# Queries and keys of an attention stage stacked through DRAM: stores of 128 partitions and loads per band in place of copies of 32 partitions

## The chip, the cores and the metric

The kernel runs on one core of a Trainium2 chip. TensorE (PE in the rows) multiplies, VectorE (DVE), ScalarE (ACT) and GpSimd (POOL) work on the elements, and SyncE (SP) issues all DMAs of the kernel from one queue. The metric is the device time of one execution in microseconds.

## The reference, cut to what matters

```python
x = x + tanh(g_xattn[0]) * xattn(layernorm(x), ctx, ctx, mask, ...)
x = x + tanh(g_ffn[0]) * ffn(layernorm(x), W_r, W_k, W_v, mu_r, mu_k)

def xattn(query, key, value, attn_mask, ...):      # B 8, S 512, D 512, 16 heads of 32
    Q, K, V = proj(query, q_w, q_b), proj(key, k_w, k_b), proj(value, v_w, v_b)
    scores = einsum('bhqd,bhkd->bhqk', Q, K) / sqrt(32)
    attn = softmax(where(attn_mask, -1e9, scores), axis=-1)
    ctx = einsum('bhqk,bhkd->bhqd', attn, V)
    return einsum('bsd,ed->bse', heads_joined(ctx), o_w) + o_b

def ffn(x, W_r, W_k, W_v, mu_r, mu_k):
    xr, xk = mu_r * x + (1 - mu_r) * x_prev, mu_k * x + (1 - mu_k) * x_prev
    return sigmoid(xr @ W_r.T) * (square(relu(xk @ W_k.T)) @ W_v.T)
```

All is float32.

## The kernel before, in words

The kernel has two stages: attention for all eight batches, then output projection and feed-forward part. The change is in the first.

A batch has four *windows* (c = 0 to 3), one for each group of four heads. A window has 16 *tiles*, and TensorE, VectorE and ScalarE each go through it in 16 *steps*: tile i = 4 * head + block of 128 queries. For each tile TensorE computes 128 x 512 scores (`scores`, L502), VectorE adds the mask and takes the row minimum (L857), ScalarE exponentiates (L681), TensorE transposes the result (L509) and VectorE or ScalarE copies it out. After the 16 steps come the context matmuls of the group (L521) and a transpose of the reciprocals (L491). `scores` runs two tiles ahead: at step 14 TensorE computes the first tile of the *next* group, and at the window's end the third.

Between the steps TensorE does *side* work by a table written by hand (`PE_SIDE`): the projections Q (L476), K (L476), V (L485) for coming groups and the transposes of x. In window 0 the parts of K for the next group stand at steps 0, 1, 3 and 4, in window 1 too, in window 2 at steps 5, 6 and 7, in window 3 at steps 0 to 2. Q for the group after the next stands at the end of a window. In window 0 the next batch's x is also loaded (L300), and VectorE takes its statistics.

Matmuls are float32r, and float32 precision is won by splitting each operand in a high and a low part. ScalarE makes the high part (`q_hi`, `k_hi`, 128 partitions for four heads x 32, and 512 columns; L670), VectorE the low part (`q_lo`, `k_lo`; L845). For scores the parts are *stacked* along the contraction: for each head a stack of 96 partitions in three bands of 32, in Q high, high, low, and in K high, low, high, so that one matmul adds the three products. There are two sets of stacks (`stack[n % 2]`). They are filled by SP: `stack_rows` (L331) copies 32 partitions of a part into one band of one head, 64 KB each, 24 copies for a group. `stacked` counts them for each head apart, and `scores` waits for a head's count at the head's first tile only (L498 to L500). `qk_hi` and `qk_lo` have no second buffer: ScalarE waits for all copies of a group before it writes the next group's part (L653, L654).

All of this stands on SP in one order, with the waits written in it:

```python
for c in range(GROUPS):
    if c == 0 and not is_last(b):
        sp.wait_ge(side_done, ...); load_x(b + 1)      # 1 MB, L300
    if c:
        store_context(b, c - 1)                        # 256 KB to DRAM, L383
    ...
        sp.wait_ge(s_mm, tile_no(b, c, 0) + HEAD)
        stack_group(b, c + 1)                          # 24 copies, L331
    if c == 0 and not is_last(b):
        load_ctx(b + 1)                                # 1 MB, L303
```

Of the kernel before, what the change touches and what calls it, by code (L numbers as in the profile page):

```python
# [25 lines left out]
P = 128  # L26
# [60 lines left out]
EARLY = LO_STEP + 1  # L87

# [17 lines left out]
STACK_DMAS = 3  # L106
# [10 lines left out]
def build(nc, x, ctxT, mask, g_xattn, g_ffn, wq, bq, wk, bk, wv, bv, wo, bo, wr, wkk, wvv, mur, muk, ident_d, out,  # L117
          ctx_dram):
# [10 lines left out]
    with keep:  # L129
# [89 lines left out]
        stacked = [[sem(f"{n}_stacked_head{j}") for j in range(GH)] for n in "qk"]  # L219
# [19 lines left out]
        def side_no(b, item):  # L239

            if b is None:
                return PROLOGUE.index(item)
            order = ORDER_LAST if isinstance(b, int) and b == B - 1 else ORDER
            return b * SIDE_PER_BATCH + len(PROLOGUE) + order.index(item)

        def side_bank_of(b, item):
            if b is None:
                return side_bank[PROLOGUE.index(item) % SIDE_BANKS]
            order = ORDER_LAST if isinstance(b, int) and b == B - 1 else ORDER
            return side_bank[(len(PROLOGUE) + order.index(item)) % SIDE_BANKS]  # L250

        def mm_no(b, item):

            order = PROLOGUE if b is None else ORDER_LAST if isinstance(b, int) and b == B - 1 else ORDER
            at = [i for i in order if i[0] != "C"].index(item)
            return at if b is None else b * MM_PER_BATCH + MM_PROLOGUE + at

        def hi_no(b, item):

            if b is None:  # L260
                return [i for i in PROLOGUE if i[0] != "V"].index(item)
            order = [i for i in (ORDER_LAST if isinstance(b, int) and b == B - 1 else ORDER) if i[0] != "V"]
            return b * HI_PER_BATCH + HI_PROLOGUE + order.index(item)
# [14 lines left out]
        def is_last(b):  # L278
            return isinstance(b, int) and b == B - 1
# [18 lines left out]
        def _(sp):  # L298
# [65 lines left out]
            stack_k(None, 0, range(GH))  # L364
            for j in range(GH):
                stack_q(None, 0, (j,))
# [18 lines left out]
            def batch(b):  # L385
                for c in range(GROUPS):
# [26 lines left out]
            for b in range(B - 1):  # L413
                batch(b)
            batch(B - 1)
# [14 lines left out]
            for b in range(B - 1):  # L430
                step2(b, 0)
                step2(b, 1)
            step2(B - 1, 0)
            step2(B - 1, 1)
# [5 lines left out]
        def _(pe):  # L440
# [124 lines left out]
            def transposes(b, h):  # L565
                u = b * 2 + h
                if isinstance(b, int) and b + h == 0:
# [10 lines left out]
            for b in range(B - 1):  # L578
                batch(b)
            batch(B - 1)  # L580
# [52 lines left out]
            for b in range(B - 1):  # L633
                step2(b, 0)
                step2(b, 1)
            step2(B - 1, 0)
            step2(B - 1, 1)
# [3 lines left out]
        def _(act):  # L641
# [4 lines left out]
            def side(b, kind, n):  # L646
# [67 lines left out]
            def early_steps(b):  # L714

                for i in range(EARLY):
                    tile_step(b, 0, i)
                    if i == HI_STEP and b:
                        side(b - 1, "R", GROUPS - 1)

            def batch(b):
                for c in range(GROUPS):
                    for i in range(EARLY if c == 0 else 0, TILES):
                        tile_step(b, c, i)
                        if is_last(b) and (c, i) in SPLIT_W2:
# [9 lines left out]
                if not is_last(b):  # L735
                    early_steps(b + 1)
# [5 lines left out]
            def context_hi(b, h):  # L742
                act.wait_ge(c2_ld[h], b * 16 + 16)
                if isinstance(b, int) and b + h == 0:

                    for copied in (*stacked[0], *stacked[1]):
                        act.wait_ge(copied, B * GROUPS * STACK_DMAS * 16)
# [3 lines left out]
            early_steps(0)  # L751
            for b in range(B - 1):
                batch(b)
            batch(B - 1)
# [42 lines left out]
            for b in range(B - 1):  # L797
                step2(b, 0)
                step2(b, 1)
            step2(B - 1, 0)  # L800
            step2(B - 1, 1)
# [3 lines left out]
        def _(dve):  # L805
# [104 lines left out]
            def early_steps(b):  # L910

                for i in range(EARLY):
                    tile_step(b, 0, i)
                    if i == LO_STEP and b:
                        side(b - 1, "R", GROUPS - 1)

            def batch(b):
                for c in range(GROUPS):
                    for i in range(EARLY if c == 0 else 0, TILES):
                        tile_step(b, c, i)  # L920
                        if c == 0 and i in STATS_STEPS and not is_last(b):
# [18 lines left out]
                if not is_last(b):  # L940
                    early_steps(b + 1)
# [5 lines left out]
            def residual1(b, h):  # L947
# [3 lines left out]
                if isinstance(b, int) and b + h == 0:  # L951
                    dve.wait_ge(consts, 3)
                if not (isinstance(b, int) and b == 0):
# [22 lines left out]
            early_steps(0)  # L976
            for b in range(B - 1):
                batch(b)
            batch(B - 1)
# [63 lines left out]
            for b in range(B - 1):  # L1043
                step2(b, 0)
                step2(b, 1)
            step2(B - 1, 0)
            step2(B - 1, 1)
# [3 lines left out]
        def _(pool):  # L1051
# [69 lines left out]
            for b in range(B - 1):  # L1121
                step2(b, 0)
                step2(b, 1)
            step2(B - 1, 0)
            step2(B - 1, 1)
# [39 lines left out]
```

## Time and profile before

| | |
|---|---|
| Time, median of 3 runs | 1234.52 us (1232.02 to 1234.85) |
| Profiled execution | 1232.68 us, of it span 1230.8 us |
| PE busy | 1167.7 us, 95% |
| DVE busy | 942.5 us, 77% |
| ACT busy | 745.2 us, 61% |
| POOL busy | 237.4 us, 19% |
| DMA moved | 110.33 MB, 90 GB/s on average |
| Chain that ended last | PE 76%, DVE 9%, issue 6%, ACT 4%, DMA 4% |
| Mean granted TensorE clock | 0.99 of full speed |

Busy is the time in which an engine had an instruction under way, as a share of the span. The chain is followed back from the last instruction, at each step to what released it. The times of all rows are microseconds from the span's start.

### The profile page before, as it was taken

To read this page: it belongs to the slowest core of one execution; us is meant where nothing else is said; L and a number is where in the kernel's file an instruction comes from. 1 tells how busy PE (TensorE), PEld (TensorE's weight loads), DVE (VectorE), ACT (ScalarE), POOL (GpSimd) and SP (SyncE) were. 2 spreads that over 40 slices of the span, in tenths; PEclk is the share of its full clock that TensorE was granted. 3 is DMA by queue.
4 is the path that set the end of the run, shared out by engine and by line. 5 is a ranking of instruction groups with operands and counts; after the bars stand their busy time and mean duration, and the time that the engine had idled before them with its cause. 6 is when DMAs were issued, how large, how long until landed. Compare 5 with 4: busy or idle time off the path is not lost.

```text
span 1230.8 us, 22178 instructions
## 1 busy us (share of the span) xinstructions
PE 1167.7 (95%) x7424; PEld 921.5 (75%) x7424; DVE 942.5 (77%) x2011; ACT 745.2 (61%) x1619; POOL 237.4 (19%) x427
## 2 busy tenths in 40 slices
PE   3999999999999999999999999977999999999997
PEld 2777776777777777777677777754888888888886
DVE  5778788788878887878878887879677677777763
ACT  4578778678768877877867876764432333233232
POOL 2030030030021003003003000024423433332431
PEclk9999999999999999999999999987999999999999
DMA  6433342253243333344225322452111311311200
GB/s 218 120 94 83 101 122 66 63 157 81 71 129 89 81 102 100 82 104 118 67 60 159 78 74 65 123 168 76 59 52 60 95 52 52 104 52 52 97 25 35
DMA packets 72703, 110.33 MB, mean 90 GB/s; under 512 B 14864, under 2 KB 23696, under 8 KB 72592
## 3 DMA queue, kind: packets, MB, share of 16 engines
q1 hardware_dynamic: 72592, 108.92, 31.1%
q8 instruction: 61, 1.00, 0.3%
q14 instruction: 50, 0.41, 0.1%
HBM read 41.76 MB, written 16.78 MB: 48 GB/s over the span
## 4 chain that ended last, share of the span: by engine, by line
PE 76%; DVE 9%; issue 6%; ACT 4%; DMA 4%; SPq 1%; POOL 0%; POOLq 0%; ACTq 0%; DVEq 0%
PE bank L445 24%; PE bank L509 14%; PE bank L476 12%; PE bank L521 10%; PE bank L502 7%; PE bank L485 6%; DMA x_rows<-x 3%; DVE neg_s L857 3%; ACT probs L681 2%; PE bank L491 2%; PE bank L575 1%; DVE pT L863 1%; DVE xh L973 1%; DMA pT<-wkT 1%; DVE ctx_sb L848 1%
## 5 line engine op out<-in xcount | busy, mean ns | idle before, releaser
L681 ACT ACTIVATE probs<-neg_s,negmax 128x512 f32<-128x512 f32 x512 | 367.9, 720 | 40.5 <-DVE negmax L857 39.4
L857 DVE CUSTOM_DVE_ANT_0 neg_s<-bank,mask_big 128x512 f32<-128x512 f32 x512 | 344.7, 683 | 19.2 <-PE bank L502 16.9
L509 PE MATMUL bank<-ident,probs 128*128 128x128 f32 x2048 | 314.8, 276 | 17.3 <-ACT probs L681 16.8
L509 PEld LDWEIGHTS bank<-ident,probs 128*128 128x128 f32 x2048 | 240.4, 141 | 75.6 <-ACT probs L681 40.7
L863 DVE COPY pT<-bank 128x512 f32<-128x512 f32 x256 | 176.5, 690 | 120.8 <-PE bank L509 119.7
L502 PE MATMUL bank<-k_stack,q_stack 96*128 96x512 f32 x512 | 243.3, 475 | 6.0 <-DVE negmax L857 5.9
L688 ACT COPY pT<-bank 128x512 f32<-128x512 f32 x256 | 149.4, 584 | 98.3 <-PE bank L509 92.5
L1068 POOL TENSOR_SCALAR var_eps<-mv 128x2 f32<-128x2 f32 (+1 forms) x24 | 18.5, 770 | 639.9 <-DVE mv L822 578.3
L521 PE MATMUL bank<-pT,v_sb 128*32 128x512 f32 x1024 | 118.5, 603 | 0.8 <-issue 0.5
L779 ACT ACTIVATE relu<-bank 128x512 f32<-128x512 f32 x32 | 19.2, 598 | 149.0 <-PE bank L445 149.0
L502 PEld LDWEIGHTS bank<-k_stack,q_stack 96*128 96x128 f32 x512 | 97.3, 190 | 11.2 <-DVE negmax L857 8.5
L681 ACT ACTIVATION_READ_ACCUMULATOR probs<-neg_s,negmax 128x1 f32 x512 | 97.3, 190 | 0.0
L521 PEld LDWEIGHTS bank<-pT,v_sb 128*32 128x32 f32 x1024 | 33.1, 111 | 69.8 <-issue 69.8
L1108 POOL TENSOR_TENSOR o_sb<-o_sb,x 128x1024 f32<-128x1024 f32 x16 | 39.1, 2444 | 173.5 <-DVE o_sb L1032 173.5
L1093 POOL TENSOR_TENSOR x_in<-x_in,tgbo 128x1024 f32<-128x1024 f32 x16 | 38.9, 2434 | 141.1 <-DMA x_in<-x 140.1
L1083 POOL TENSOR_SCALAR x_rows<-x_rows,mv,rstd 128x512 f32<-128x512 f32 x28 | 57.8, 2078 | 0.8
L476 PE MATMUL bank<-cT_lo,wk_hi 128*128 128x512 f32 x128 | 40.4, 418 | 17.2 <-DVE cT_lo L836 17.2
L672 ACT COPY ctx_sb<-bank 128x512 f32<-128x512 f32 x32 | 18.8, 589 | 62.4 <-PE bank L491 62.4
L1017 DVE TENSOR_TENSOR kact_lo<-kact,kact_hi 128x1024 fp32r<-128x1024 f32 x16 | 40.0, 2498 | 17.9 <-ACT kact_hi L781 17.9
L957 DVE SCALAR_TENSOR_TENSOR x<-bank,tg,x_in 128x512 f32<-128x512 f32 x32 | 23.9, 751 | 37.1 <-POOL o_sb L1108 35.9
L1014 DVE SCALAR_TENSOR_TENSOR kact<-bank,relu 128x512 f32<-128x512 f32 x32 | 22.1, 692 | 38.5 <-ACT relu L779 38.5
L485 PE MATMUL bank<-wv_hi,cT_lo 128*128 128x256 f32 x256 | 45.6, 282 | 0.0
(110 smaller groups left out, 2125.1 us busy)
## 6 DMA issues: line engine op xcount, KB each, us to landing
k_stack<-k_hi SPq DMA_DIRECT2D x256, 64.0 KB, 2.0
q_stack<-q_hi SPq DMA_DIRECT2D x256, 64.0 KB, 2.0
x_rows<-x SPq DMA_DIRECT2D x8, 1024.0 KB, 6.6
cT_raw<-ctxT SPq DMA_DIRECT2D x8, 1024.0 KB, 5.8
k_stack<-k_lo SPq DMA_DIRECT2D x128, 64.0 KB, 2.0
q_stack<-q_lo SPq DMA_DIRECT2D x128, 64.0 KB, 2.0
ctx_dram<-ctx_sb SPq DMA_DIRECT2D x32, 256.0 KB, 2.1
c_raw<-ctx_dram SPq DMA_DIRECT2D x16, 512.0 KB, 5.1
```

The costliest lines, as they stand in the source:

```text
L445: mm = nc.tensor.matmul(dst, lhs(left, a), rhs(right, a), start=(part == 0 and a == 0), stop=(part == TERMS - 1 and a == CH - 1))
L476: mm = nc.tensor.matmul(bank[:], left[:, at % CH, cols], right[:, at % CH, :], start=(at == 0), stop=(at == TERMS * CH - 1))
L485: mm = nc.tensor.matmul(bank[:, k * UNIT:(k + 1) * UNIT], left[:, a, keys * P:(keys + 1) * P], right[:, a, n // 2 * UNIT:(n // 2 + 1) * UNIT],
L502: nc.tensor.matmul(s_bank[i % S_BANKS][:], stack[slot][0][:, j, q * P:(q + 1) * P], stack[slot][1][:, j, :], start=True, stop=True).then_i ...
L509: mm = nc.tensor.transpose(pt_bank[i % 2][:, a * P:(a + 1) * P], probs[:, i % P_RING, a * P:(a + 1) * P], ident[:])
L521: nc.tensor.matmul(pv_bank[j * HD:(j + 1) * HD, :], v_sb[:, a, head * HD:(head + 1) * HD], pT[:, j, a, :], start=(a == 0), stop=(a == TT - 1))
L681: nc.scalar.activation(probs[:, i % P_RING, :], neg_s[:, i % SM_RING, :], ACT.Exp, bias=negmax[:, k:k + 1], scale=-1.0, accum_out=den[:, g ...
L688: nc.scalar.copy(pT[:, j, :, q * P:(q + 1) * P], blocks(pt_bank[i % 2])).then_inc(pt_out[1], 1)
L857: nc.vector.tensor_tensor_reduce(neg_s[:, i % SM_RING, :], s_bank[i % S_BANKS][:], mask_big[:, q, :], 1.0, 3e38, ALU.add, ALU.min, negmax[ ...
L863: nc.vector.tensor_copy(pT[:, j, :, q * P:(q + 1) * P], blocks(pt_bank[i % 2])).then_inc(pt_out[0], 1)
L1017: nc.vector.tensor_tensor(kact_lo[:].rearrange("p a t -> p (a t)"), kact[:].rearrange("p m d -> p (m d)"), kact_hi[:].rearrange("p a t -> ...
L1083: nc.gpsimd.tensor_scalar(x_rows[:, t, :], x_rows[:, t, :], mv[:, t, 0:1], rstd[:, t:t + 1], ALU.subtract, ALU.mult).then_inc(xhat_done, 1)
```

## The change

A new DRAM tensor, `qk_dram`, holds each part of each group. `store_part` stores a whole part (128 partitions, 256 KB) to it; `load_bands` waits until that store has landed, and then loads one band for all four heads at once (32 partitions x 4 heads x 512, 256 KB). A group has four stores and six loads. The counts change with it: `stacked` is one semaphore for Q and one for K, raised by three loads each; `scores` waits for both counts at the first tile of a group; ScalarE's next `q_hi` and `k_hi` wait for the stores (`part_st`) and not for the stacks. Q's stores no longer wait for the window's start, its loads do. K's high part is stored before its low part is ready. The store of the context moves behind the stacks. `early_steps` goes away and the loops are written plainly, which leaves the order on the compute engines as it was.

```diff
-            def stack_rows(kind, n, bands, source, heads):
-                dst = stack[n % 2]["QK".index(kind)]
-                copied = stacked["QK".index(kind)]
-                for j in heads:
-                    for band in bands:
-                        sp.dma_start(dst[HD * band:HD * (band + 1), j, :].bitcast(F32),
-                                     source[HD * j:HD * (j + 1), :].bitcast(F32)).then_inc(copied[j], 16)
+            def store_part(g, which, part):
+                source = (qk_hi, qk_lo)[part][which]
+                sp.dma_start(qk_dram[g, which, part], source[:].bitcast(F32)).then_inc(part_st[which][part], 16)
+
+            def load_bands(g, which, part):
+                sp.wait_ge(part_st[which][part], (g + 1) * 16)
+                for band in range(BANDS):
+                    if ((0, 0, 1), (0, 1, 0))[which][band] == part:
+                        sp.dma_start(stack[g % 2][which][HD * band:HD * (band + 1), :, :].bitcast(F32),
+                                     qk_dram[g, which, part].rearrange("(j d) t -> d j t", j=GH)).then_inc(stacked[which], 16)
...
-            def stack_q(b, n, heads):
+            def store_q(b, n):
+                g = b * GROUPS + n
                 sp.wait_ge(side_hi, q_hi_count(b, n))
-                stack_rows("Q", n, (0, 1), qk_hi[0], heads)
+                store_part(g, 0, 0)
                 sp.wait_ge(side_done, q_lo_count(b, n))
-                stack_rows("Q", n, (2,), qk_lo[0], heads)
-
-            def stack_k(b, n, heads):
+                store_part(g, 0, 1)
+
+            def store_k(b, n):
+                g = n if b is None else b * GROUPS + n
+                sp.wait_ge(side_hi, hi_no(b, ("K", n)) + 1)
+                store_part(g, 1, 0)
                 sp.wait_ge(side_done, done(side_no(b, ("K", n))))
-                for j in heads:
-                    stack_rows("K", n, (0, 2), qk_hi[1], (j,))
-                    stack_rows("K", n, (1,), qk_lo[1], (j,))
+                store_part(g, 1, 1)
...
             def stack_group(b, n):
-                first = GH if n == GROUPS - 1 else GH - 1
-                stack_q(b, n, range(first))
-                stack_k(b, n, (0,))
-                if first < GH:
-                    stack_q(b, n, (first,))
-                stack_k(b, n, range(1, GH))
+                g = b * GROUPS + n
+                store_q(b, n)
+                sp.wait_ge(s_mm, (g - 1) * TILES + HEAD)
+                load_bands(g, 0, 0)
+                load_bands(g, 0, 1)
+                store_k(b, n)
+                load_bands(g, 1, 0)
+                load_bands(g, 1, 1)
...
-                    if c:
-                        store_context(b, c - 1)
                     if not (is_last(b) and c == GROUPS - 1):
-                        sp.wait_ge(s_mm, tile_no(b, c, 0) + HEAD)
...
                         stack_group(b, c + 1)
+                    if c:
+                        store_context(b, c - 1)
...
-                if i % TT == 0:
+                if i % TILES == 0:
                     for copied in stacked:
-                        pe.wait_ge(copied[j], (b * GROUPS + c + i // TILES + 1) * STACK_DMAS * 16)
+                        pe.wait_ge(copied, (b * GROUPS + c + i // TILES + 1) * BANDS * 16)
...
-                    for copied in stacked["QK".index(kind)]:
-                        act.wait_ge(copied, ((0 if b is None else b * GROUPS) + n) * STACK_DMAS * 16)
+                    for stored in part_st["QK".index(kind)]:
+                        act.wait_ge(stored, ((0 if b is None else b * GROUPS) + n) * 16)
```

On SP, from the load of the next x in window 0 on, this stood before; a name in brackets is the semaphore waited for:

```order
L300 DMA x_rows<-x 128x4x512 [waits side_done]
L331 DMA q_stack<-q_hi 32x512 [waits side_hi,s_mm]
L331 DMA q_stack<-q_hi 32x512 x5
L331 DMA q_stack<-q_lo 32x512 [waits side_done]
L331 DMA q_stack<-q_lo 32x512 x2
L331 DMA k_stack<-k_hi 32x512 [waits side_done]
L331 DMA k_stack<-k_hi 32x512
L331 DMA k_stack<-k_lo 32x512
L331 DMA q_stack<-q_hi 32x512 [waits side_hi]
```

and this stands there now, up to the load of the next context input (L302; line numbers are those of the changed kernel):

```order
L299 DMA x_rows<-x 128x4x512 [waits side_done]
L327 DMA qk_dram<-q_hi 128x512 [waits side_hi]
L327 DMA qk_dram<-q_lo 128x512 [waits side_done]
L334 DMA q_stack<-qk_dram 32x4x512 [waits q_hi_st,s_mm]
L334 DMA q_stack<-qk_dram 32x4x512
L334 DMA q_stack<-qk_dram 32x4x512 [waits q_lo_st]
L327 DMA qk_dram<-k_hi 128x512 [waits side_hi]
L327 DMA qk_dram<-k_lo 128x512 [waits side_done]
L334 DMA k_stack<-qk_dram 32x4x512 [waits k_hi_st]
L334 DMA k_stack<-qk_dram 32x4x512
L334 DMA k_stack<-qk_dram 32x4x512 [waits k_lo_st]
L302 DMA cT_raw<-ctxT 128x4x512
```

K's first copy stood behind nine copies that wait for nothing but Q; now K's stores stand behind Q's loads, and these behind the landing of Q's stores.

On TensorE, around the first scores of the next group (step 14 of a window 0), this stood before:

```order
L476 MATMUL bank<-xT_hi,wq_lo 128x512 x2
L509 MATMUL bank<-ident,probs 128x128 [waits pt_out_act,p_exp]
L509 MATMUL bank<-ident,probs 128x128 x3
L502 MATMUL bank<-k_stack,q_stack 128x512 [waits s_min,k_stacked_head0,q_stacked_head0]
L476 MATMUL bank<-xT_hi,wq_lo 128x512 x2
```

and this stands there now:

```order
L483 MATMUL bank<-xT_hi,wq_lo 128x512 x2
L516 MATMUL bank<-ident,probs 128x128 [waits pt_out_act,p_exp]
L516 MATMUL bank<-ident,probs 128x128 x3
L509 MATMUL bank<-k_stack,q_stack 128x512 [waits s_min,k_stacked,q_stacked]
L483 MATMUL bank<-xT_hi,wq_lo 128x512 x2
```

The order is the same; the wait was for head 0's copies and is now for the whole group's.

## Rows read from the trace of the kernel before

**Rows 1.** The page: busy us (share of the span) x instructions

```profile
PE 1167.7 (95%) x7424; PEld 921.5 (75%) x7424; DVE 942.5 (77%) x2011; ACT 745.2 (61%) x1619; POOL 237.4 (19%) x427
```

**Rows 2.** Busy time by stretch, attention stage

```profile
core 0: us, PE busy (x) PEld busy (x) DVE busy (x) ACT busy (x) POOL busy (x), PEclk, DMA share, GB/s
...
30.00:860.00 830.00, 796.99 (x5400) 606.17 (x5400) 668.38 (x1610) 616.24 (x1442) 101.07 (x153) 0.99 0.36 97
```

**Rows 3.** Who waited for whom: us in total, times, longest

```profile
ACT q_hi L670 <- DMA q_stack<-q_lo: 3.0, 1, 3.0
```

**Rows 4.** Timeline of SP, window 0 of batch 2: start, us, line

```profile
245.55 0.43 SPq L300 DMA_DIRECT2D x_rows<-x  x1
246.08 3.69 SPq L331 DMA_DIRECT2D q_stack<-q_hi  x6
```

**Rows 5.** Landing of the x load (L300), then of the first Q copy (L331), there

```profile
DMA to landing us min/median/max: 6.2/6.2/6.2
...
DMA to landing us min/median/max: 5.6/5.6/5.6
```

**Rows 6.** The page, DMA issues: count, KB each, median us to landing

```profile
q_stack<-q_hi SPq DMA_DIRECT2D x256, 64.0 KB, 2.0
x_rows<-x SPq DMA_DIRECT2D x8, 1024.0 KB, 6.6
...
ctx_dram<-ctx_sb SPq DMA_DIRECT2D x32, 256.0 KB, 2.1
```

**Rows 7.** Timeline of TensorE, end of window 0 of batch 2

```profile
257.16 0.47 PE L502 MATMUL bank<-k_stack,q_stack 96*128 96x512 f32 x1
...
259.44 0.66 PE L509 MATMUL bank<-ident,probs 128*128 128x128 f32 x4 [0.35 <-ACT probs L681]
...
260.95 3.64 PE L521 MATMUL bank<-pT,v_sb 128*32 128x512 f32 x32
```

**Rows 8.** Timeline of VectorE, window 0 of batch 2

```profile
248.13 0.75 DVE L845 SCALAR_TENSOR_TENSOR k_lo<-bank,bk_col,k_hi 128x512 fp32r<-128x512 f32 x1
```

**Rows 9.** The same, batch 6 (issue, landing, scores), then batch 0

```profile
645.88 0.43 SPq L300 DMA_DIRECT2D x_rows<-x  x1
...
DMA to landing us min/median/max: 6.9/6.9/6.9
...
658.14 0.48 PE L502 MATMUL bank<-k_stack,q_stack 96*128 96x512 f32 x1
...
42.20 0.39 SPq L300 DMA_DIRECT2D x_rows<-x  x1
...
57.75 0.48 PE L502 MATMUL bank<-k_stack,q_stack 96*128 96x512 f32 x1
```

**Rows 10.** Timelines of SP and TensorE, window 2 of batch 2

```profile
301.93 1.14 SPq L331 DMA_DIRECT2D k_stack<-k_hi  x2
...
306.36 0.47 PE L502 MATMUL bank<-k_stack,q_stack 96*128 96x512 f32 x1
```

**Rows 11.** Stage change: TensorE's timeline, stretches, VectorE's c_lo, POOL's timeline

```profile
818.31 2.04 PE L445 MATMUL bank<-w2o_lo,c_hi 128*128 128x512 f32 x4 [4.47 <-DVE ctx_sb L848]
...
824.29 1.09 PE L445 MATMUL bank<-w2o_hi,c_hi 128*128 128x512 f32 x4
...
847.31 5.66 PE L521 MATMUL bank<-pT,v_sb 128*32 128x512 f32 x32
...
818.30:821.00 2.70, 2.69 (x9) 2.21 (x9) 1.68 (x5) 0.81 (x2) 0.00 (x0) 0.50 1.05 388
833.00:836.00 3.00, 1.00 (x5) 0.44 (x4) 3.00 (x9) 2.24 (x3) 0.93 (x5) 1.00 0.41 151
...
L945 DVE TENSOR_TENSOR c_lo<-c_raw,c_hi x16: 1209/1214/3216, 814.3 to 1176.6; 128x1024 fp32r<-128x1024 f32 x16
...
814.14 2.34 POOL L1093 TENSOR_TENSOR x_in<-x_in,tgbo 128x1024 f32<-128x1024 f32 x1 [139.82 <-DMA x_in<-x]
```

**Rows 12.** Prologue: timelines of VectorE and TensorE

```profile
30.65 0.75 DVE L845 SCALAR_TENSOR_TENSOR q_lo<-bank,bq_neg,q_hi 128x512 fp32r<-128x512 f32 x1 [1.85 <-ACT tg L704]
...
35.34 0.63 PE L502 MATMUL bank<-k_stack,q_stack 96*128 96x512 f32 x2
```

More of the change, by code:

```diff
@@ L218, in build @@
         side_mm, side_hi, side_done = sem("side_mm"), sem("side_hi"), sem("side_done")
-        stacked = [[sem(f"{n}_stacked_head{j}") for j in range(GH)] for n in "qk"]
+        part_st = [[sem(f"{n}_{part}_st") for part in ("hi", "lo")] for n in "qk"]
+        stacked = [sem(f"{n}_stacked") for n in "qk"]
         s_mm, s_min, p_exp, p_tr = sem("s_mm"), sem("s_min"), sem("p_exp"), sem("p_tr")
@@ L411, in batch @@
                 store_context(b, GROUPS - 1)
-            for b in range(B - 1):
+            for b in range(B):
                 batch(b)
-            batch(B - 1)
             for s in range(2):
@@ L428, in step2 @@
                              o_sb[:, h]).then_inc(out_st[h], 16)
-            for b in range(B - 1):
+            for b in range(B):
                 step2(b, 0)
                 step2(b, 1)
-            step2(B - 1, 0)
-            step2(B - 1, 1)
             for s in range(2):
@@ L576, in transposes @@
                     mm.then_inc(t_mm, 1)
-            for b in range(B - 1):
+            for b in range(B):
                 batch(b)
-            batch(B - 1)
             def o_proj(b, h):
@@ L631, in step2 @@
                     o_proj(b + 1, h)
-            for b in range(B - 1):
+            for b in range(B):
                 step2(b, 0)
                 step2(b, 1)
-            step2(B - 1, 0)
-            step2(B - 1, 1)
         @block.scalar
@@ L712, in tile_step @@
                     probs_out(b, c, i)
[L714 to L719, printed above, removed]
             def batch(b):
                 for c in range(GROUPS):
-                    for i in range(EARLY if c == 0 else 0, TILES):
+                    for i in range(TILES):
                         tile_step(b, c, i)
+                        if b and (c, i) == (0, HI_STEP):
+                            side(b - 1, "R", GROUPS - 1)
                         if is_last(b) and (c, i) in SPLIT_W2:
@@ L743, in context_hi @@
                 act.wait_ge(c2_ld[h], b * 16 + 16)
-                if isinstance(b, int) and b + h == 0:
-                    for copied in (*stacked[0], *stacked[1]):
-                        act.wait_ge(copied, B * GROUPS * STACK_DMAS * 16)
+                if b + h == 0:
+                    for stored in (*part_st[0], *part_st[1]):
+                        act.wait_ge(stored, B * GROUPS * 16)
                 act.wait_ge(o_mm, (b * 2 + h) * UM)
                 nc.scalar.copy(c_hi[:], c_raw[:, h]).then_inc(c2_hi, 1)
-            early_steps(0)
-            for b in range(B - 1):
+            for b in range(B):
                 batch(b)
-            batch(B - 1)
             def xT_out(b, h):
@@ L796, in _ @@
             mixed_hi(0, 0, 1)
-            for b in range(B - 1):
+            for b in range(B):
                 step2(b, 0)
                 step2(b, 1)
-            step2(B - 1, 0)
-            step2(B - 1, 1)
         @block.vector
@@ L908, in tile_step @@
                     probs_out(b, c, i)
[L910 to L915, printed above, removed]
             def batch(b):
                 for c in range(GROUPS):
-                    for i in range(EARLY if c == 0 else 0, TILES):
+                    for i in range(TILES):
                         tile_step(b, c, i)
+                        if b and (c, i) == (0, LO_STEP):
+                            side(b - 1, "R", GROUPS - 1)
                         if c == 0 and i in STATS_STEPS and not is_last(b):
@@ L950, in residual1 @@
                 dve.wait_ge(xb_done, u + 1)
-                if isinstance(b, int) and b + h == 0:
+                if b + h == 0:
                     dve.wait_ge(consts, 3)
-                if not (isinstance(b, int) and b == 0):
+                if not (b == 0):
                     dve.wait_ge(o_done, u - 1 + HEAD)
@@ L974, in normalise2 @@
                                             ALU.subtract, ALU.mult).then_inc(xh_done, 1)
-            early_steps(0)
-            for b in range(B - 1):
+            for b in range(B):
                 batch(b)
-            batch(B - 1)
             def difference(b, h):
@@ L1042, in _ @@
             mixed_lo(0, 0, 0)
-            for b in range(B - 1):
+            for b in range(B):
                 step2(b, 0)
                 step2(b, 1)
-            step2(B - 1, 0)
-            step2(B - 1, 1)
         @block.gpsimd
@@ L1120, in _ @@
             split_w2(3)
-            for b in range(B - 1):
+            for b in range(B):
                 step2(b, 0)
                 step2(b, 1)
-            step2(B - 1, 0)
-            step2(B - 1, 1)
 def kernel(x, ctx_1024, mask_SxS2_bk1, g_xattn, g_ffn, L0_xattn_q_w, L0_xattn_q_b, L0_xattn_k_w, L0_xattn_k_b,
```

36 lines of the change are left out of this document (19 added, 17 removed).

## The prediction

> **What bounds the kernel now.** I read the page first: the busy shares [rows 1]. TensorE is busy 95% of the span. The attention stage (30 to 860 us, by the windows view) has TensorE busy 797 of 830 us [rows 2]: whatever makes TensorE stand still there lengthens the kernel nearly one for one. Then the waits, for what the stacks cost now: one line, ScalarE's q_hi waiting 3.0 us for the last copy, once, in the prologue [rows 3]; TensorE's waits name VectorE and ScalarE. So the 24 copies of a group are hidden today, although SP spends 0.62 us on each (3.69 us for six [rows 4]), some 15 us for a group. What the change can win on the copies is therefore small; the question is when the last stack lands, and when TensorE asks for it.
>
> TensorE asks for the stacks of the next group at step 14 of a window (scores looks two tiles ahead). Before, it asks there only for head 0; the other heads are asked for 4, 8 and 12 steps later. After, one count stands for all bands and heads, so everything must be there at step 14.
>
> *Window 0* (batch 2 as the example). SP issues the 1 MB x load at 245.55, and at 246.08 the Q copies [rows 4]. The first Q copy lands 5.6 us after issue, at 251.7, beside the x load's 6.2 us [rows 5], against 2.0 us for an undisturbed copy [rows 6]: what is issued behind x lands behind x. Step 14's scores start at 257.16, and TensorE is idle only 0.35 us between 258 and 261 [rows 7]. K's low part is done at 248.9 [rows 8]; K is not the late one, the queue is. From x landing (251.8) to scores there are 5.4 us. Batch 6 reads the same: x issued at 645.88, landed 6.9 us later, scores at 658.14, so 5.4 us; these are two of the six batches 1 to 6, all between 5.3 and 5.4. Batch 0, with x issued at 42.20 and the scores at 57.75, has 15.6 us between them where batch 2 has 11.6 [rows 9].
>
> *Window 2.* K's projection is late here (steps 5 to 7). SP gets the low part at 301.93 and TensorE wants the stack at 306.36 [rows 10], less 0.15 for loading weights: 4.3 us. In windows 1 and 3 the low part of K comes out 8 and 10 steps ahead of step 14, in place of 5, and no x load lies in front.
>
> **The change part by part.** (a) *24 copies become 4 stores and 6 loads.* Nothing on a compute engine changes, only waits. SP's issue time drops by some 10 us a group, worth nothing where SP isn't waited for.
>
> (b) *K's way gets a second leg.* A copy lands in 2.0 us. Now a store must land before its load is issued. A 256 KB store: the context store, same shape, 2.1 us [rows 6]. A load of 256 KB onto 32 partitions isn't in the trace. Below: 2.0, as the 64 KB copy onto 32 partitions. Above: by a line from 2.0 for 64 KB to 6.6 for the 1 MB load [rows 6], 2.9 us. I take 2.4, between them. Window 2: 2.1 + 2.4 = 4.5 against 4.3, so a stall of 0.3 us (0 to 0.9), eight times: **+2.4 us** (0 to 7).
>
> (c) *Window 0: five transfers in a row.* From x landing: the q_hi store lands behind it, +0.6 (nothing, as for the first Q copy, to 1.2, which the line of (b) gives for 256 KB); three Q loads issued, 3 x 0.5 (x takes 0.43, a copy 0.62 [rows 4]); two K stores issued, 0.4 each; landing 2.1, or 0.9 later if they queue behind the Q loads; three K loads issued, the last one 1.0 after the first; it lands 2.0 after issue, or 3.6 with the two before it in the way. Counted out for batch 2: Q store landed at 251.8 to 253.0, Q loads issued by 253.3 to 254.5, K's high part landed at 255.4 to 257.5, last K load issued at 256.4 to 258.5, landed at 258.4 to 262.1. TensorE wants it at 257.0: a stall of 1.4 to 5.1, I take the middle, 3.3. The 0.35 us for which it waits for ScalarE right after [rows 7] is caught up in the stall: 3.0 net. Batches 1 to 6: **+18 us** (6 to 29). Batch 0 has 4 us more room and comes out at about zero; batch 7 loads no x.
>
> (d) *The clock.* At the stage change TensorE is idle for 4.47 us, and comes back at a granted clock of 0.50 of full speed, 1.2 in place of 2.4 GHz: four matmuls of the O projection take 2.04 us, and 1.09 once the clock is back; the context matmuls there take 5.66 us [rows 11] and 3.64 at full speed [rows 7]. It falls again after a stretch with only 1.0 us busy of 3 (833 to 836 [rows 11]); 0.35 us of idle left it alone [rows 7]. A stall of 3.3 us is nearer to the two that made it fall. The cost: 2.0 for the context matmuls, and up to 0.8 for Q's last six matmuls and the transposes ahead of them; I take 2.4, six times: **+14.4 us**, or none if it doesn't fall. The Trainium skill (TensorE: Matmul & The Clock Gate, the HAM clock gate) says that the throttled state is the default and activity lifts it, which agrees with these rows; a kernel in which the gate stayed open would be my second case below.
>
> (e) *Prologue.* Q's stack comes through two legs: q_lo done 31.4, stored 33.5, loaded about 36, against scores at 35.34: +0.6 [rows 12]. But q_hi of the next group waits only for the stores and not 3.0 us for the copies [rows 3], and TensorE then idles less: **-1 us** net.
>
> (f) *Stage change.* The next stage's loads stand behind the last K copies on SP and move some 4.5 us forward. POOL's x_in addition ran beside VectorE's c_lo, which took 3.22 us where its median is 1.21 [rows 11]; earlier it would be over by then: **-2 us** (0 to -5, if TensorE's shorter idle also spares the clock).
>
> (g) *Waits.* ScalarE's q_hi and k_hi wait for stores instead of copies: earlier, never waited for beyond (e). The context store moves behind the stacks on SP; its ring has two windows of room, so nothing.
>
> Sum: 2.4 + 18 + 14.4 - 1 - 2 = **+31.8**. The profiled execution took 1232.7 us (span 1230.8 and 1.9 around it), the median of the three runs is 1234.5, 1.8 above: 1264.5 against the one, and I say 1265.
>
> The Trainium skill (DMA: Bandwidth & Descriptors, Anatomy of one DMA) gives a fit of about 2.0 us plus bytes over 436 KB/us, so an estimate of 2.6 us for each leg. The store's row says 2.1, so that leg disagrees; with 2.6 twice, window 2 would stall 0.9 us and give 7 us in place of 2.4. The sum stays with the rows.
>
> **The rivals.**
> *A, my forecast:* stalls in window 0 with the clock falling: 1248 (6 + 12 - 3) to 1285 (29 + 17 + 7 - 1). 0.57.
> *B, the same stalls, clock stays up:* 1232.7 + 17.4 = 1250 (1236 to 1266). For it: short idles left the clock alone; against: the stretch at 833 to 836. 0.22.
> *C, hidden:* the transfers overlap more than I count (Q stores not held up by x, issue times of 0.35) so that the last K load lands by 257. That needs 1.4 us less than my lowest count, which is against it: 1232 to 1237, same. 0.08.
> *D, faster:* C's condition, and the prologue and the stage change give back 3 to 7 us: 1226 to 1230. Its place is 3.0 us of ScalarE's wait and 2.0 us of c_lo with the half-clock steps behind it; it decides only if window 0 stalls by less than 0.5 us. The Trainium skill (same page, Rules for kernel authors) speaks for it: many small transfers should be coalesced, since under 64 KB one pays mostly overhead. The rows agree that 64 KB and 256 KB land alike (2.0 and 2.1), but that overhead is hidden here. 0.06.
> *E, worse:* loads onto 32 partitions land later than 3.6 us in a burst of three, or stall windows 1 and 3 too: above 1285. 0.07.
>
> **How the numbers follow.** A run tells a change from none at about 0.3%, 4 us. Slower: A, B and E, 0.86. Same: C, 0.08. Faster: D, 0.06. The time is A's. The range, 1237 to 1284, takes in nearly all of A and B and leaves out C, D and E.
>
> **What would show it.** In the waits, TensorE's scores line waiting for a k_stack load, 14 times or so: some 3 us in window 0 of batches 1 to 6 and below 1 us in each window 2. The clock view: half speed right after the long ones. On SP's queue, the K stores issued 2 us or more after x has landed. The context matmuls of window 0 longer than 3.64. c_lo near 1.2 us. I am wrong if window 0's scores don't wait, if the band loads land far from 2.0 to 3.6 us, or if a wait shows in windows 1 or 3.

## The result: 6.7% slower, where 2.5% was forecast

| | median | lowest to highest | ratio to the kernel before (95%) |
|---|---|---|---|
| before | 1233.42 us (4 runs) | 1232.02 to 1234.85 | |
| changed | 1317.14 us (4 runs) | 1310.72 to 1320.59 | 1.067 [1.065, 1.070] |

The profiled execution of the changed kernel took 1310.7 us, its span is 1308.9. First the page of the profile after, busy us and share; it answers to [rows 1].

```profile
span 1308.9 us, 21570 instructions
PE 1184.4 (90%) x7424; PEld 935.3 (71%) x7424; DVE 942.5 (72%) x2011; ACT 746.6 (57%) x1619; POOL 237.7 (18%) x427
```

The span grew by 78.1 us. TensorE does the same 7424 matmuls in 16.7 us more of busy time, at a mean granted clock of 0.968 for 0.990, and is idle for 61.4 us more. Where it idles, the waits of the scores line say: us in total, times, the longest.

```profile
PEld bank L509 <- issue: 69.5, 16, 8.6
PE bank L509 <- issue: 66.2, 16, 8.4
...
DVE neg_s L850 <- PE bank L509: 85.2, 59, 8.0
```

"issue" means that the profile names no releaser. The 16 waits are step 14 of windows 0 and 2 of all eight batches, where `scores` waits for both stacks; the timeline shows them, in brackets (batch 2, window 0, then window 2):

```profile
287.90 0.77 PE L509 MATMUL bank<-k_stack,q_stack 96*128 96x512 f32 x1 [7.74 <-issue]
...
340.00 0.47 PE L509 MATMUL bank<-k_stack,q_stack 96*128 96x512 f32 x1 [1.77 <-issue]
```

Over the batches windows 0 wait 2.59, 8.37, 7.74, 6.89, 6.57, 6.31, 7.45 and 2.36 us, 48.3 in all; windows 2 wait 1.91, 3.40, 1.77, 1.77, 1.83, 1.72, 3.35 and 2.15, 17.9 in all. Windows 1 and 3 don't wait for their stacks. SP's timeline of the same window 0 answers to [rows 4]:

```profile
267.83 0.34 SPq L395 DMA_DIRECT2D ctx_dram<-ctx_sb  x1
268.21 0.43 SPq L299 DMA_DIRECT2D x_rows<-x  x1
268.69 0.57 SPq L327 DMA_DIRECT2D qk_dram<-q_hi  x1
269.30 0.44 SPq L327 DMA_DIRECT2D qk_dram<-q_lo  x1
275.27 2.53 SPq L334 DMA_DIRECT2D q_stack<-qk_dram  x3
277.85 0.43 SPq L327 DMA_DIRECT2D qk_dram<-k_hi  x1
278.32 0.43 SPq L327 DMA_DIRECT2D qk_dram<-k_lo  x1
281.84 1.27 SPq L334 DMA_DIRECT2D k_stack<-qk_dram  x3
```

Here the chain of five can be read off: x landed at 274.5 (6.3 us after issue), Q's high part at 275.2, Q's loads were issued by 277.8, K's high part landed at 281.8, 4.0 us after its issue, K's last load was issued at 282.7 and landed 5.1 us later, at 287.8. TensorE started 0.1 us after that. The page's list of DMAs answers to [rows 6]:

```profile
k_stack<-qk_dram SPq DMA_DIRECT2D x96, 256.0 KB, 3.9
q_stack<-qk_dram SPq DMA_DIRECT2D x96, 256.0 KB, 4.0
x_rows<-x SPq DMA_DIRECT2D x8, 1024.0 KB, 6.3
...
qk_dram<-k_hi SPq DMA_DIRECT2D x32, 256.0 KB, 2.0
```

A band load lands in 3.9 to 4.0 us at the median. I had taken 2.4 for one alone.

### The profile page after: what moved, and what is told of

Read it like the earlier page. It is cut to its first block, busy times and chain, and to the rows that moved or that the text cites. A ratio compares the mean times of both kernels' runs of the same rounds, so it can differ in the third digit from the quotient of the medians.

```text
span 1308.9 us, 21570 instructions
## 1 busy us (share of the span) xinstructions
PE 1184.4 (90%) x7424; PEld 935.3 (71%) x7424; DVE 942.5 (72%) x2011; ACT 746.6 (57%) x1619; POOL 237.7 (18%) x427
## 4 chain that ended last, share of the span: by engine, by line
PE 75%; issue 10%; DMA 5%; DVE 5%; ACT 3%; SPq 1%; POOL 0%; POOLq 0%; ACTq 0%; DVEq 0%
PE bank L452 23%; PE bank L516 15%; PE bank L483 13%; PE bank L528 9%; PE bank L509 8%; PE bank L492 6%; DMA q_stack<-qk_dram 2%; DMA qk_dram<-q_hi 2%; PE bank L498 1%; PE bank L582 1%; DVE neg_s L850 1%; ACT probs L685 1%; DVE xh L959 1%; DMA qk_dram<-q_lo 1%; DMA pT<-wkT 1%
## 5 line engine op out<-in xcount | busy, mean ns | idle before, releaser
L516 PE MATMUL bank<-ident,probs 128*128 128x128 f32 x2048 | 320.3, 280 | 13.5 <-ACT probs L685 13.3
L509 PE MATMUL bank<-k_stack,q_stack 96*128 96x512 f32 x512 | 248.6, 486 | 74.3 <-issue 66.2
L516 PEld LDWEIGHTS bank<-ident,probs 128*128 128x128 f32 x2048 | 247.7, 144 | 69.3 <-ACT probs L685 31.2
L483 PE MATMUL bank<-cT_lo,wk_hi 128*128 128x512 f32 x128 | 40.4, 418 | 16.7 <-DVE cT_lo L829 16.7
L1001 DVE TENSOR_TENSOR kact_lo<-kact,kact_hi 128x1024 fp32r<-128x1024 f32 x16 | 39.9, 2493 | 17.9 <-ACT kact_hi L776 17.9
L483 PE MATMUL bank<-xT_hi,wq_hi 128*128 128x512 f32 x128 | 46.4, 448 | 0.0
```

What stands on the lines that cost most here:

```text
L483: mm = nc.tensor.matmul(bank[:], left[:, at % CH, cols], right[:, at % CH, :], start=(at == 0), stop=(at == TERMS * CH - 1))
L509: nc.tensor.matmul(s_bank[i % S_BANKS][:], stack[slot][0][:, j, q * P:(q + 1) * P], stack[slot][1][:, j, :], start=True, stop=True).then_i ...
L516: mm = nc.tensor.transpose(pt_bank[i % 2][:, a * P:(a + 1) * P], probs[:, i % P_RING, a * P:(a + 1) * P], ident[:])
L1001: nc.vector.tensor_tensor(kact_lo[:].rearrange("p a t -> p (a t)"), kact[:].rearrange("p m d -> p (m d)"), kact_hi[:].rearrange("p a t -> ...
```

## The experiments

The theory after this result: the stacks come late because band loads take longer than I gave them, each alone and more so in a row, and because in window 0 they stand in one queue with x and with K's stores. The rivals: reading DRAM is what is slow; the coarse wait is to blame, not the DMAs; the clock.

### DMAs alone

Only SP works in these two kernels, and each group of DMAs is waited for before the next; the computation is left out.

> This kernel leaves the whole computation out and only issues DMAs, each kind three or four times, one after the other with a wait for landing between: a 256 KB store of 128 partitions, a 256 KB band load (32 partitions x 4 x 2 KB), a 256 KB load onto 128 partitions, a 64 KB copy and a 64 KB load onto 32 partitions, three band loads at once, two band loads onto partitions 0 to 63, two onto 0 to 31 and 64 to 95, three loads of 128 partitions at once, and a 1 MB load. Theory (the 32 partitions make a band load slow): a single band load lands in about 3.1 us and the third of three in about 5, while a 256 KB load onto 128 partitions lands near 2.3 and the third of three near 3.5; two bands that lie in 0 to 63 land later than two that lie in 0 to 31 and 64 to 95. Rival (reading DRAM is what is slow, on however many partitions): the load onto 128 partitions lands at 3.1 too, and the 64 KB load from DRAM well above the 2.0 us of the copy. My forecast had 2.0 to 2.9 for one band load, up to 3.6 for the last of three.

What landed, in us at the median, by the list of DMAs (`one_band` is a band load, `wide` a load onto 128 partitions, `thin` the copy of before, `thin_dram` its counterpart from DRAM):

```profile
dram<-part SPq DMA_DIRECT2D x4, 256.0 KB, 2.0
one_band<-dram SPq DMA_DIRECT2D x4, 256.0 KB, 3.0
...
thin<-part SPq DMA_DIRECT2D x4, 64.0 KB, 2.0
thin_dram<-dram SPq DMA_DIRECT2D x4, 64.0 KB, 1.8
```

The four single loads onto 128 partitions, then the three bursts of three band loads, then the three bursts of three onto 128 partitions, each lowest, median and highest:

```profile
DMA to landing us min/median/max: 2.6/2.7/2.7
...
DMA to landing us min/median/max: 2.9/3.9/4.4
...
DMA to landing us min/median/max: 2.7/3.0/3.7
```

DRAM as such isn't slow: 64 KB from it land in 1.8 us, sooner than the copy. 256 KB take 0.9 us more onto 128 partitions, and 0.3 on top of that onto 32. In a burst the difference grows: the third band load lands after 4.3 to 4.4 us, the third wide one after 3.6 to 3.7 (4.1 in the next run, with two stores behind it). What the DMA engines move shows it too, GB/s in 40 slices, first over bursts of band loads (54 to 69 us), then over bursts of wide ones (94 to 106 us):

```profile
GB/s 60 0 0 0 169 251 344 306 213 219 218 240 137 0 0 0 0 0 82 251 426 235 213 213 208 279 175 16 0 0 0 0 208 246 328 306 235 180 218 257
...
GB/s 0 0 0 0 14 41 89 396 403 396 403 328 341 116 82 14 0 0 0 102 116 137 382 410 382 246 239 218 191 191 7 0 0 0 0 82 198 396 389 403
```

A slice is 0.3 or 0.4 us. Band loads peak early in each burst (328 to 426 GB/s) and then run mostly at 208 to 240; the first wide burst stays at 328 to 403 until its last slices, the second falls from 410 to between 191 and 246. Pairs of bands on partitions 0 to 63 landed at 3.5 at the median and pairs on 0 to 31 and 64 to 95 at 3.3, so which bands they are matters little. Neither theory has all of it: for one load the size takes most and the shape the rest (2.7 us onto 128 partitions, where the theory had 2.3); in a burst the shape costs more.

> Again only DMAs, the computation is left out: three band loads with two 256 KB stores issued right behind them; three loads of 128 partitions with two stores behind; a 1 MB load with two stores behind; six band loads at once; three times each. Theory (one queue in order, so a store waits for the bytes of the loads ahead of it): the stores behind three band loads land in 3.5 to 4.2 us in place of 2.0, behind three loads of 128 partitions 0.5 us or so sooner, behind the 1 MB load in 5 to 6; the last of six band loads lands 6 to 7 us after its issue. Rival (the 4.0 us of K's stores in the changed kernel come from something else, such as reading a buffer just written, or the engines' own traffic): alone on the chip they land in 2.0 to 2.6 behind the band loads.

Two stores right behind three band loads, lowest, median and highest landing, and then the last two of six band loads in a row:

```profile
DMA to landing us min/median/max: 4.5/4.6/4.6
...
DMA to landing us min/median/max: 5.9/6.1/6.4
```

A store that lands in 2.0 us alone takes 4.5 to 4.7 behind three band loads, 3.7 to 4.5 behind three wide ones, and 6.0 behind 1 MB. That is more than the theory's 3.5 to 4.2. So the 4.0 us of K's stores in the changed kernel need no other cause than the queue. The six band loads land 1.0 to 1.3 us apart while they are issued 0.43 us apart: that pace is what a burst costs.

### K's stores ahead of Q's loads

```diff
                 store_q(b, n)
+                if n == 1:
+                    store_k(b, n)
                 sp.wait_ge(s_mm, (g - 1) * TILES + HEAD)
                 load_bands(g, 0, 0)
                 load_bands(g, 0, 1)
-                store_k(b, n)
+                if n != 1:
+                    store_k(b, n)
```

> The changed kernel with K's two stores moved ahead of Q's three loads on SP, in window 0 only. Theory (window 0 stalls on a chain of transfers, each held up by those before it): K's stores land within about 2 us after x and no longer take 4.0; the last band load lands some 2 to 3.5 us sooner, the stalls of window 0 fall from 6.3 to 8.4 us to 4 to 5.5, and the time falls by 12 to 20 us, to 1297 to 1305. Rival (the band loads themselves fill the time: six in a row at 1.2 us and more): the same bytes pass the same way, the stall falls by under 1 us and the time by under 6.

1294.1 us, ratio 1.052 [1.049, 1.054]: 23 us less than the changed kernel by the medians, 16.3 by the two spans, 13.1 of it in the waits of windows 0 of batches 1 to 6, which fell from 43.3 to 30.2 us in all. The stalls fell to 3.8 to 5.6 us, about where the theory had them, and the time a little further than its 12 to 20 us. But the stalls didn't go, since six band loads now stand in a row.

### x a window earlier

```diff
+            load_x(1)
+
...
-                    if c == 0 and not is_last(b):
-                        sp.wait_ge(side_done, done(b * SIDE_PER_BATCH + len(PROLOGUE) - 1))
-                        load_x(b + 1)
...
                         stack_group(b, c + 1)
+                    if c == GROUPS - 1 and b + 2 < B:
+                        load_x(b + 2)
```

> The changed kernel with the load of the next x issued one window earlier, behind the stacks of window 3 (and for batch 1 in the prologue), so that nothing lies ahead of the stacks in window 0. Theory (the 1 MB load in front is what makes window 0 late): the 48 us of stalls in the eight windows 0 go to nearly nothing and the clock stays up there, 1252 to 1262 us; window 2 keeps its 18 us. Rival (store plus load is too long for any window, or the band loads are slowed by something else): window 0 keeps stalls of over 2 us and the time stays above 1275.

1274.6 us, 1.035 [1.032, 1.038], 42.5 less by the medians and 35.3 by the two spans. That missed the theory's 1252 to 1262: x in front was the larger part of window 0's loss (48.3 us of stalls became 20.4), yet stalls of 2.3 to 4.7 us were left in the windows 0 of batches 1 to 6, and 2.2 in batch 7. SP's timeline shows why: Q's low part was ready at 249.7, but its store stands behind the context store of the batch before, which isn't ready until 257.3; and K's stores stand behind Q's loads again, 4.5 us from issue (261.39) to the first load that they release (265.91).

```profile
257.29 0.33 SPq L397 DMA_DIRECT2D ctx_dram<-ctx_sb  x1
257.66 0.43 SPq L327 DMA_DIRECT2D qk_dram<-q_hi  x1
...
260.08 1.27 SPq L334 DMA_DIRECT2D q_stack<-qk_dram  x3
261.39 0.43 SPq L327 DMA_DIRECT2D qk_dram<-k_hi  x1
...
265.91 2.00 SPq L334 DMA_DIRECT2D k_stack<-qk_dram  x3
```

### Work in the stall

```diff
+                if i == TILES and c == 0 and 0 < b < B - 1:
+                    pe.wait_ge(side_done, previous_r(b, c))
+                    for _ in range(26):
+                        nc.tensor.matmul(pv_bank[:], act_hi[1][:, 0, 0:P], act_hi[1][:, 0, :], start=True, stop=True)
```

> The changed kernel with 26 matmuls of 128 x 512 whose result nobody reads, put on TensorE just ahead of the waiting scores in window 0 of batches 1 to 6: 5.7 us of work inside a stall of 6.3 to 8.4 us. They take nothing away from the wait and keep TensorE busy. Theory (2.4 us a batch are lost to the clock after the stall): the clock stays at full speed over windows 0, the context matmuls stay at 3.64 us, and the time falls by 8 to 15 us. Rival (the clock costs nothing beside the wait, or ScalarE and VectorE set the time after it): within 3 us of the changed kernel. If the matmuls run over the stall the time rises instead.

1303.3 us, 1.058 [1.055, 1.061]: 11 us less by the ratios, 14 by the medians and 7 by the two profiled spans, with 156 matmuls more. The mean granted clock over the span rose from 0.968 to 0.984 (0.990 before the change). The wait itself was hardly touched: from step 14 of window 3 to step 14 of the next window 0, six times, it is 191.5 us for 192.5. What was won lies behind the stall. From step 14 of window 0 to that of window 1 the changed kernel takes 25.0 to 26.0 us in batches 1 to 6, and with the stall filled 23.5 in five of them (25.1 in batch 1, where the clock fell in spite of the fill): 9.5 us in all. In the changed kernel it looks like this (stretch, busy times, then PEclk): 14 us that begin 2.1 us before the end of batch 1's stall, within them the context matmuls, and the stall itself.

```profile
172.00:186.00 14.00, 11.95 (x69) 7.78 (x70) 6.11 (x19) 4.08 (x9) 6.10 (x17) 0.77 0.58 164
179.29:182.93 3.64, 3.64 (x34) 1.00 (x34) 1.81 (x5) 1.34 (x3) 2.62 (x13) 1.00 0.37 144
...
165.69:174.06 8.37, 0.01 (x1) 0.04 (x1) 1.14 (x3) 1.47 (x5) 0.00 (x0) 0.65 0.88 230
```

The context matmuls (x34 with two neighbours) already run at 1.00; the low clock begins in the stall and ends ahead of them.

### Both orders, and then K's projection earlier

> Both orders of before together: x loaded a window earlier and K's stores ahead of Q's loads in window 0. With x moved alone, window 0 kept stalls of 1.9 to 4.7 us: SP stored Q at 257.7, loaded it, then stored K at 261.4, and these stores took 4.0 us to land. Theory (that queue is all that is left): K's stores land some 3 us sooner and the stalls of window 0 go to under 1 us, windows 2 keep 1.6 to 3.4 us each; 1252 to 1261 us. Rival (six band loads in a row cannot be done in the time that a window 0 leaves): stalls of 2 us and more stay in window 0 and the time stays within 5 us of 1274.

1263.0 us, 1.025 [1.022, 1.027]. That is 2 us above the theory's range, and its stall "under 1 us" was wrong: all eight windows 0 still wait, 1.3 to 2.7 us. All six loads now go out in a row:

```profile
259.73 1.36 SPq L334 DMA_DIRECT2D q_stack<-qk_dram  x3
261.13 1.38 SPq L334 DMA_DIRECT2D k_stack<-qk_dram  x3
...
DMA to landing us min/median/max: 6.5/6.8/7.2
...
269.39 0.47 PE L511 MATMUL bank<-k_stack,q_stack 96*128 96x512 f32 x1 [1.60 <-issue]
```

The last is issued at about 262.1 and lands 7.2 us later, at 269.3; the scores start at 269.39. Alone, the last of six band loads lands 6.3 to 6.4 us after its issue. So the pace of a burst explains about half of this stall of 1.6 us; the other 0.8 us, for which the loads land later than alone, stay open. Then the order of TensorE's side work in window 2 as well:

```diff
-    {step: [("T", n, 0, 1)] for n, step in enumerate((0, 1, 3, 4))} | parts("K", 3, 5, 6, 7)
-    | parts("Q", 4, 9, 10, 12, 13, 14, 16),
+    parts("K", 3, 0, 1, 3) | {step: [("T", n, 0, 1)] for n, step in enumerate((4, 5, 6, 7))}
+    | parts("Q", 4, 10, 11, 12, 13, 14, 16),
```

> The stacks through DRAM as in the changed kernel, with x earlier, K's stores ahead of Q's loads in window 0, and in window 2 the parts of K's projection at steps 0, 1 and 3, with the transposes of x behind them at steps 4 to 7 and Q's projection at 10 to 16. Theory (window 2 stalls only because K's low part comes 4.4 us before the scores, and a store and the third of three band loads take 6.1): K's low part comes some 5 us sooner, the stalls of windows 2 go to zero and 13 to 18 us are won against 1263, to 1245 to 1252; about 1.7 us a window 0 stay for the six band loads in a row. Rival (the new order costs TensorE what it wins, since Q's projection now waits for the transposes of x): windows 2 lose 1 us and more elsewhere and the time stays above 1255.

1246.4 us, 1.013 [1.011, 1.015], 16.6 less, within the theory's range, and its scores line has 8 waits, all in windows 0:

```profile
  issue: 14.4, 8
```

So the stalls of windows 2 (17.9 us in the changed kernel, 16.0 in the run before this one) come from the place of K's projection: with the low part earlier they are gone.

### Half of the change, and the coarse wait by itself

Q as in the changed kernel, K by the 12 copies of before with a wait for each head:

```diff
-                store_k(b, n)
-                load_bands(g, 1, 0)
-                load_bands(g, 1, 1)
+                copy_k(b, n)        # 12 copies, as stack_k before
...
+                if i % TT == 0:
+                    pe.wait_ge(k_copied[j], (b * GROUPS + c + i // TILES + 1) * BANDS * 16)
```

> Half of the change: Q's stacks through DRAM as in the changed kernel, K's by the 12 copies of before, with a wait for each head. Theory (what costs in window 2 is K's second leg, what costs in window 0 is the chain of five transfers): window 2 stalls no more, window 0 loses the K store and its landing, so the copies of head 0 are issued at once behind Q's loads and stall TensorE 1 to 3 us in place of 6.3 to 8.4; 1244 to 1258 us. Rival (Q's route is what holds everything up, whatever K does): windows 0 keep 5 us and more, the time stays above 1275.

1242.1 us, 1.007 [1.006, 1.009], 2 us under the theory's range. Windows 2 don't stall, windows 0 of batches 1 to 6 stall 1.4 to 2.1 us. So nearly nine tenths of the loss hang on K's half of the change. This edit gives K back both its copies and its wait for each head, and doesn't tell the two apart.

> Q's stacks through DRAM, K's by copies with a wait for each head, and x a window earlier. In the half change window 0 still stalled 1.4 to 2.1 us in six batches. Theory (only x in front of Q's stores made it late): no stall is left in windows 0, and 10 to 14 us are won against 1242, to 1228 to 1233, level with the kernel before or up to 0.4% faster. Rival (SP's 12 copies behind Q's loads are late by themselves): stalls above 1 us stay and the time stays above 1237.

The same with the edit of the second experiment: 1230.3 us, 0.9995 [0.998, 1.001], level with the kernel before, as the theory said; no window stalls.

The kernel before with one wait for all heads:

```diff
-                if i % TT == 0:
-                    for copied in stacked:
-                        pe.wait_ge(copied[j], (b * GROUPS + c + i // TILES + 1) * STACK_DMAS * 16)
+                if i % TILES == 0:
+                    for copied in (*stacked[0], *stacked[1]):
+                        pe.wait_ge(copied, (b * GROUPS + c + i // TILES + 1) * STACK_DMAS * 16)
```

> The kernel before, with only the wait made coarse: at a group's first scores TensorE waits for the copies of all four heads. Theory (the 24 copies of before are hidden only by the wait for each head): the last copy of K is issued at 261.6 in window 0 and lands 2 us later, 6.5 us after the scores want to start, and about 5 us late in window 2 and 5 to 6 in window 1, so the kernel loses 100 to 150 us, 1330 to 1380. Rival (the coarse wait is harmless and DRAM alone is to blame): under 1245 us.

1425.4 us in its one run, more than the theory said. All 31 windows that are followed by another group stall, by 2 to 6 us and 130.5 us in all; TensorE's busy time grew by another 62.4 us, at a mean granted clock of 0.939, which the theory left out. Windows 0 and 1 of batch 2:

```profile
284.24 0.47 PE L502 MATMUL bank<-k_stack,q_stack 96*128 96x512 f32 x1 [2.65 <-DMA k_stack<-k_lo]
316.20 0.76 PE L502 MATMUL bank<-k_stack,q_stack 96*128 96x512 f32 x1 [5.82 <-DMA k_stack<-k_lo]
```

So the 24 copies were hidden by the wait for each head. The changed kernel gives that up; its loads are fewer and done sooner than 24 copies, but all must land, since each carries one band of all four heads. Loads for one head at a time with a wait for each, or loads issued by a second engine, were not run: how much of the changed kernel's loss a finer wait would save is not shown.

### The order that beats both

> The kernel before, with nothing changed but the next x loaded one window earlier (behind the copies of window 3, and in the prologue for batch 1). Theory (before, the stacks were in time in every window, so x in front of them cost TensorE almost nothing): window 0 takes about 1 us longer than window 1 in the kernel before, for VectorE's wait for x; at most that comes back, 1 to 6 us in all, 1227 to 1233. Rival (the x load in front of the copies cost before too, as it does after the change): 10 us and more are won.

The kernel before with x a window earlier: 1227.8 us in 12 runs against 1231.1 in 23, ratio 0.9971 [0.9956, 0.9986]. It is the fastest of all, by 0.3% and within the theory's range, and that is all that x in front of the copies cost before.

## Why the prediction was right and wrong

**Right: the mechanism and its places.** Step 14 of windows 0 and 2 stalls, and windows 1 and 3 don't. The budget of window 0 nearly held: 5.4 us from x landing to scores [rows 4 to 9], and 5.7 in batch 2 now (274.5 to 280.2, where the scores wait begins). The first step of the chain of five transfers was right too, +0.7 for the Q store behind x, where 0.6 was said.

**The failed step is the landing of the transfers in (b) and (c).** The two stalls were to cost 20.4 us and cost 66.2 (17.9 in windows 2, 48.3 in windows 0). With some 11 us for the clock behind windows 0 that is 77 us, and the span grew by 78.1.

**Wrong: the size of terms (b) and (c), by one price.** I bounded the landing of a band load by 2.0 and 2.9 us, took 2.4, and gave the last of a burst of three at most 3.6. Alone it takes 3.0, in the kernel 3.9 at the median, and the third of three 4.3 to 5.1. The line through [rows 6] had 1.2 us for each further 256 KB, and that is about the pace which a burst keeps (1.0 to 1.3). I used it as an upper bound for a single load and not as the pace of a row of them. Term (b): 17.9 us of stall for 2.4. With the measured legs, 2.0 + 4.3 - 4.4 gives 1.9, and most windows 2 show 1.7 to 1.9. In batches 1 and 6 they stall 3.4. The third load took 6.0 us in batch 1, and in batch 6 the second one held SP for 1.59 us; why stays open.

**Wrong: what stands behind the Q loads.** Term (c) let K's stores land in 2.1 to 3.0 us; they took 4.0. Q's three loads were to be issued in 1.5 us and took 2.5, as the second one held SP for 1.70 us. Why is open: alone a load holds it for 0.43. K's last load took 5.1 for 2.0 to 3.6. So batch 2's window 0 stalls 7.7 us in place of 3.3. Against the middle of my count Q's loads make 1.1 of these 4.4 us, K's stores 1.4 and K's last load 2.3, less some 0.4 by which the scores came later. In all that is 43.3 us in batches 1 to 6 for 18, and 2.6 and 2.4 in batches 0 and 7, for which I had said zero.

**Right in kind, near in size by luck: (d), the clock.** It falls in the stalls, and 14.4 us were said where 7 to 14 came back when TensorE was kept busy. But 2.0 of my 2.4 us a window were to be lost in the context matmuls, and those take 3.64 us, as before, in all six windows:

```profile
292.56 3.64 PE L528 MATMUL bank<-pT,v_sb 128*32 128x512 f32 x32
```

The cost lies ahead of them. The scores behind the stall take 0.77 us for 0.47, and the context matmuls begin 4.7 to 5.6 us after those scores; with the stall filled they begin after 3.14 us in five of the six batches. That is 1.5 to 2.5 us a window, 11 in all, and it was paid behind stalls of 6 to 8 us, while I had priced one of 3.3. The sign that I had named, longer context matmuls, didn't come.

The Trainium skill (TensorE: Matmul & The Clock Gate, the HAM clock gate) says that activity releases the throttle. The filled stalls agree, in five windows of six.

**Wrong, small: (e).** The prologue was to give 1 us and cost about 2. TensorE waited 2.5 us for Q's stack there for 0.6, and the next x load was issued at 44.14, 1.9 us later than before [rows 9].

**Right, and given back in part: (f).** c_lo takes 1.2 us for 3.2, and TensorE's idle time ahead of the O projection fell from 4.47 [rows 11] to 2.48. That is the 2 us that were said. But the addition on POOL now runs at the time of w2o_lo, which takes 3.30 us for 2.29 before:

```profile
897.87 1.31 PE L452 MATMUL bank<-w2o_lo,c_hi 128*128 128x512 f32 x4 [2.48 <-DVE ctx_sb L841]
...
888.45 2.39 POOL L1075 TENSOR_TENSOR x_in<-x_in,tgbo 128x1024 f32<-128x1024 f32 x1 [143.63 <-DMA x_in<-x]
...
889.69 3.30 DVE L922 TENSOR_TENSOR w2o_lo<-w_raw,w2o_hi 128x2048 fp32r<-128x2048 f32 x1 [1.77 <-ACT w2o_hi L737]
```

**The Trainium skill's fit** for one DMA (DMA: Bandwidth & Descriptors, Anatomy of one DMA) gave an estimate of 2.6 us a leg. The page measured it on DMAs that GpSimd issues, which I hadn't said; SP issues these. A single load onto 128 partitions took 2.7, a store 2.0. My sum set the fit aside on the store's row; for the load, which no row showed, it would have been nearer, though still under the 3.0 of a band load.

**The rival that came true is E**, with 0.07: "later than 3.6 us in a burst of three".

## What to carry to other kernels

When many small transfers become a few large ones, ask first who waits, and for how much of it: 24 copies, 15 us in all, lay hidden behind a wait for each head, and six loads of a few microseconds don't behind one wait for all. Cost a burst by its pace and not by the landing of one, and give each transfer on a queue the bytes ahead of it, stores too. What stands just ahead of the urgent transfers in one queue (here 1 MB of x) may be able to go earlier: one window earlier won 42 us in the changed kernel and 3 us in the kernel before. And look at the matmuls behind a stall: here the low clock cost another 1.5 to 2.5 us behind each stall of 6 us and more.

## What the runs showed of the hardware

A 256 KB load takes 2.7 us onto 128 partitions and 3.0 onto 32, while a 256 KB store takes 2.0 and 64 KB from DRAM 1.8. Six band loads in a row land 1.0 to 1.3 us apart, about 220 KB/us. Bursts of loads onto 32 partitions settle at 208 to 240 GB/s, one onto 128 partitions kept 328 to 403, another fell to 191 to 246. A store of 2.0 us takes 4.5 to 4.7 us behind three such loads. In the kernel before SP is held 0.59 us at the median by a copy of 32 partitions within SBUF (0.51 to 0.57 when it works alone), and 0.3 to 0.43 us by a load or store of four times its size that works alone; in the changed kernel single loads hold it for up to 2.0 us.
